# Turning only the normed tokens of a block, by products with the identity into both halves of the partitions

## The chip, the cores and the metric

The kernel runs on one core of one Trainium2 chip. The metric is the device time of one execution in microseconds: three runs of the kernel before took 3504.92, 3515.65 and 3518.93 us, median 3515.65. The profile is of a fourth execution, which took 3525.21 us.

## The reference

The input is a batch of 32 images of 56 x 56 pixels with 64 channels, in fp32. The last of three stages is the one that matters here, a mixture of experts over all 100,352 tokens:

```python
x = x + relu(conv3x3(group_norm(x), binary_kernel))
t = tokens(x)
t = t + linear_attention(layer_norm(t))          # 8 heads, per pair of images
xf = layer_norm(t)
top_w, top_i = top_k(xf @ Wg + bg, 2); top_w = softmax(top_w)
for e in range(8):
    h = gelu(xf @ W1[e] + b1[e])                 # 64 -> 256
    out = out + w_dense[:, e:e+1] * (h @ W2[e] + b2[e])   # 256 -> 64
t = t + out
```

Every token uses two of the eight experts, so it falls into one of 28 classes (pairs of experts).

## The kernel before, in words

Images are worked on in 16 pairs. For each pair the kernel does the convolution, the attention, the second layer norm and the gate, then sorts the tokens by class and scatters them as rows into a table in device memory (`rows`). A row has 132 columns: 0 to 63 the token itself, 64 to 127 its normed form (`COL_X` to `COL_W`), then the two weights and the token's number. Rows of one class fill blocks of 512 tokens (`BLK`), and each block passes through its two experts.

A block (functions `turn_in`, `hidden`, `outputs`, `turn_out` on TensorE; `turned`, `gelu`, `evacuate` on ScalarE) goes as follows. SyncE loads the block's rows (`xb`, 128 partitions x 4 tokens x 132) and the two experts' weights. `turn_in` transposes four groups of 128 tokens, each a 128 x 128 piece of token and normed token, into one PSUM bank: the normed tokens come out in partitions 64 to 127. `turned` copies that half twice, into partitions 0 to 63 and 64 to 127 of `xts` in SBUF, because the two experts' hidden products use the two halves of TensorE's rows. `hidden` (two halves q of the 256 hidden units) multiplies by W1, ScalarE applies gelu, `outputs` multiplies by W2, `evacuate` copies the result, `turn_out` transposes it back into the same PSUM bank that `turn_in` uses (`TB`), and VectorE combines it with the weights and adds the token. GpSimd scatters the result, four DMAs a block.

There are 224 blocks. 156 of them run in thirteen turns of 12 blocks (the text calls such a turn of the outer loop a TURN), in a fixed order between the steps of the pairs that come behind them: `STEPS` and `BLOCK_STEPS` give every step a place on every engine, and each engine works through its own list in that order, waiting on semaphores. So a block's turn in can stand between steps of the attention or the convolution of another pair. The other 68 blocks run alone in a tail, written out block by block, with functions of their own (`in_tail`, `hidden_tail`, `outputs_tail`, `out_tail`, `tail_x`, `gelu_tail`): there the turn in (L1041) has a PSUM bank of its own, and TensorE's order within a block is hidden product 0, turn in of the next block, output product 0 of the block before, hidden product 1, output product 1, turn out.

Lines: L990 and L1041 turn in, L800 and L801 (turns) and L825 and L826 (tail) the copies to `xts`, L972 and L1023 hidden products, L981 and L1032 output products, L998 and L1049 turn out, L788 and L818 gelu, L884 convolution, L871 turning the input of the convolution, L894 turning its output, L899 and L907 keys, queries and values, L913, L920, L926, L935 the rest of the attention, L942 and L949 the gate's logits, L707 squares of the layer norms. L640 is GpSimd's scatter of results, L634 that of sorted rows.

## Time and profile before

| | us |
|---|---|
| median of three runs | 3515.65 |
| lowest and highest | 3504.92, 3518.93 |
| profiled execution | 3525.21 |
| its span, first to last instruction | 3523.1 |
| TensorE busy | 3018.8 (86%) |
| VectorE busy | 2232.3 (63%) |
| ScalarE busy | 1885.4 (54%) |
| GpSimd busy | 1873.1 (53%) |
| mean granted TensorE clock | 0.914 |

The granted clock is a share of TensorE's full speed; 1.0 is 2.4 GHz and the other level is 0.5. A matmul's busy time in the profile includes the time that its result takes to come out, so the distance from one start to the next says more of TensorE's throughput than the mean duration. The first 700 us have no blocks, 700 to 3130 us hold the thirteen TURNs, and from 3130 us on the tail runs.

### The profile page before, as it was taken

To read this page: it belongs to the slowest core of one execution; us is meant where nothing else is said; L and a number is where in the kernel's file an instruction comes from. 1 tells how busy PE (TensorE), PEld (TensorE's weight loads), DVE (VectorE), ACT (ScalarE), POOL (GpSimd) and SP (SyncE) were. 2 spreads that over 40 slices of the span, in tenths; PEclk is the share of its full clock that TensorE was granted. 3 is DMA by queue.
4 is the path that set the end of the run, shared out by engine and by line. 5 is a ranking of instruction groups with operands and counts; after the bars stand their busy time and mean duration, and the time that the engine had idled before them with its cause. 6 is when DMAs were issued, how large, how long until landed. Compare 5 with 4: busy or idle time off the path is not lost. (4 is left out here: it accounts for less than half of the span.)

```text
span 3523.1 us, 60494 instructions
## 1 busy us (share of the span) xinstructions
PE 3018.8 (86%) x16878; PEld 1610.9 (46%) x16878; DVE 2232.3 (63%) x5060; ACT 1885.4 (54%) x3186; POOL 1873.1 (53%) x1837
## 2 busy tenths in 40 slices
PE   3787787889898989999898989899998977579997
PEld 2554554554544444545445444445454443123332
DVE  3677768676868586767667585867677667122222
ACT  2424243365655556565656465565656445347776
POOL 0006244264646556473737465464747375757777
PEclk8888787899999999999999999899999898889999
DMA  8303313142524252433424252424333222234442
GB/s 224 83 26 108 91 64 102 56 121 69 145 72 134 78 137 82 122 88 99 112 83 129 65 142 70 133 80 119 90 108 93 84 74 57 75 92 132 123 104 61
DMA packets 406811, 345.90 MB, mean 98 GB/s; under 512 B 258189, under 2 KB 347028, under 8 KB 400656
## 3 DMA queue, kind: packets, MB, share of 16 engines
q1 hardware_dynamic: 343632, 260.62, 28.0%
q0 software_dynamic: 53760, 78.84, 6.6%
q10 hardware_dynamic: 9088, 2.47, 0.4%
q8 instruction: 153, 2.51, 0.3%
q14 instruction: 178, 1.46, 0.1%
HBM read 261.66 MB, written 147.47 MB: 116 GB/s over the span
## 5 line engine op out<-in xcount | busy, mean ns | idle before, releaser
L634 POOL DMA_INDIRECT rows<-R,place_at x784 | 802.8, 1024 | 571.7 <-issue 513.7
L640 POOL DMA_INDIRECT out<-o_sb,xb x624 | 664.0, 1064 | 722.5 <-DVE o_sb L1471 406.2
L788 ACT ACTIVATE h_sb<-psum,w2b 128x512 f32<-128x512 f32 x624 | 394.2, 683 | 329.3 <-PE psum L972 327.6
L884 PE MATMUL psum<-xpad,conv_w 128*64 128x448 f32 x2688 | 546.4, 558 | 10.0 <-ACT xpad L717 7.5
L972 PE MATMUL psum<-xts,w1b 64*128 64x512 f32 x1248 | 386.4, 693 | 61.0 <-ACT h_sb L788 31.4
L981 PE MATMUL psum<-h_sb,w2b 128*64 128x512 f32 x1248 | 353.4, 646 | 48.0 <-ACT h_sb L788 47.5
L884 PEld LDWEIGHTS psum<-xpad,conv_w 128*64 128x64 f32 x2688 | 190.5, 140 | 329.0 <-issue 315.0
L640 POOL DMA_INDIRECT out<-o_sb,xpad x272 | 272.0, 1000 | 119.2 <-issue 92.7
L751 ACT ACTIVATE conv_y<-psum 128x448 f32<-128x448 f32 x112 | 60.5, 541 | 367.4 <-PE psum L884 367.4
L907 PE MATMUL psum<-WT,conv_y 128*112 128x256 f32 x896 | 233.8, 393 | 11.6 <-DVE QT L1394 6.5
L616 POOL TENSOR_TENSOR QT<-QT,q_sum 112x512 f32<-112x512 f32 x112 | 120.5, 1082 | 229.3 <-DVE q_sum L1419 228.0
L742 ACT COPY xpad<-psum 128x448 f32<-128x448 f32 x224 | 142.8, 648 | 180.8 <-PE psum L871 179.7
L1483 DVE TENSOR_TENSOR y_w<-psum,xpad 128x512 f32<-128x512 f32 x68 | 47.0, 692 | 270.9 <-PE psum L1049 267.0
L818 ACT ACTIVATE h_sb<-psum,VT 128x512 f32<-128x512 f32 x272 | 172.2, 684 | 79.0 <-PE psum L1032 71.5
L871 PE MATMUL psum<-ident,raw 112*128 112x112 f32 x896 | 145.0, 302 | 80.3 <-DMA raw<-in_x 30.0
L894 PE MATMUL psum<-ident,conv_y 128*64 128x64 f32 x3136 | 198.9, 287 | 12.4 <-DVE x_tok L1378 11.7
L894 PEld LDWEIGHTS psum<-ident,conv_y 128*64 128x64 f32 x3136 | 185.8, 205 | 49.8 <-issue 30.3
L907 PEld LDWEIGHTS psum<-WT,conv_y 128*112 128x112 f32 x896 | 151.7, 179 | 109.9 <-issue 48.9
L972 PEld LDWEIGHTS psum<-xts,w1b 64*128 64x128 f32 x1248 | 104.0, 198 | 212.7 <-issue 157.6
L926 PE MATMUL psum<-KT,VT 112*128 112x128 f32 x896 | 140.1, 314 | 55.3 <-ACT KT L729 55.3
L717 ACT ACTIVATE xpad<-xpad,gn 128x784 f32<-128x784 f32 (+2 forms) x160 | 160.1, 1034 | 30.9 <-DVE gn L1370 30.2
L871 PEld LDWEIGHTS psum<-ident,raw 112*128 112x128 f32 x896 | 107.6, 162 | 142.0 <-issue 75.3
(230 smaller groups left out, 5572.3 us busy)
## 6 DMA issues: line engine op xcount, KB each, us to landing
rows<-rows SPq DMA_DIRECT2D x236, 264.0 KB, 5.8
xb<-rows SPq DMA_DIRECT2D x156, 264.0 KB, 2.7
x_tok<-in_x SPq DMA_DIRECT2D x16, 1568.0 KB, 7.3
w2b<-w2x SPq DMA_DIRECT2D x312, 65.0 KB
w1b<-w1x SPq DMA_DIRECT2D x312, 64.2 KB
xpad<-rows SPq DMA_DIRECT2D x68, 264.0 KB, 2.7
raw<-in_x SPq DMA_DIRECT2D x32, 448.0 KB
raw<-in_x SPq DMA_DIRECT2D x32, 440.0 KB
```

What stands on the lines that cost most here:

```text
L634: pool.indirect_dma_start(rows[:, :], bass.IndirectOffsetOnAxis(ap=place_at[:, j:j + 1], axis=0), R[:, j, :], None) \
L640: pool.indirect_dma_start(out_rows, bass.IndirectOffsetOnAxis(ap=block_rows[:, t, COL_ID:COL_ID + 1].bitcast(U32), axis=0), tokens[:, t, : ...
L717: ins = act.activation(part, part, ACT.Identity, bias=shift[h, :], scale=scale[h, :])
L742: act.copy(dst, src[:, 0:448].rearrange("p (k r h) -> p r h k", k=4, h=2)) \
L788: act.activation(h_sb[:, e, q, :], psum[:, HB0 + e, :], ACT.Gelu, bias=w2b[:, i, e, 2 * C + q:2 * C + q + 1]).then_inc(S["h_ready"], 1)
L818: act.activation(h_sb[:, e, q, :], psum[:, HB0 + 2 * q + e, :], ACT.Gelu, bias=t_w2[:, k % TAIL_RING, e, 2 * C + q:2 * C + q + 1]).then_in ...
L871: ins = pe.transpose(dst[:, TQ * r:TQ * r + TQ], raw[0:TQ, 4 * grp + r, :], ident[0:TQ, 0:TQ])
L884: ins = pe.matmul(dst[64 * i:64 * i + 64, 0:BL], conv_w[:, t, :], xpad[:, i, r0:r0 + ROWS, dx:dx + HW], start=(t == 0), stop=(t == 5))
L894: ins = pe.matmul(dst[h, C * j:C * j + C], cols[:, JB * b + j, :], ident[:, h], start=True, stop=True)
L907: ins = pe.matmul(dst[0:LC, 256 * c:256 * c + 256], t[:, o:o + LC], WT4[:, 0:2, :].rearrange("p w m -> p (w m)"), start=True, stop=True)
L972: ins = pe.matmul(psum[:, HB0 + e, :], w1b[h, i, 128 * q:128 * q + 128], xts[h, i % 2, :], start=True, stop=True)
L981: ins = pe.matmul(psum[64 * e:64 * e + 64, YB, :], w2b[:, i, e, C * q:C * q + C], h_sb[:, e, q, :], start=(q == 0), stop=(q == 1))
```

## The change

`turn_in` and `in_tail` no longer transpose 128 x 128 pieces. For each of the four groups of 128 tokens they take only the 64 normed columns as the stationary operand and the identity as the moving one, and multiply twice: once into partitions 0 to 63 of the PSUM bank and once into 64 to 127. Both halves then hold the turned normed tokens, and ScalarE copies all 128 partitions at once.

```diff
             def turned(q4, i):
                 act.wait_ge(*blocks_done("xt_full", (q4, i), 1, 1))
                 act.wait_ge(*blocks_done("h_full", block_at(q4, i - 2), 2, 2))
-                act.copy(xts[0:C, i % 2, :], psum[COL_X:COL_W, TB, :])
-                act.copy(xts[C:128, i % 2, :], psum[COL_X:COL_W, TB, :]).then_inc(S["xt_free"], 1)
+                act.copy(xts[:, i % 2, :], psum[:, TB, :]).then_inc(S["xt_free"], 1)
...
-                act.copy(xts[0:C, k % 2, :], psum[COL_X:COL_W, T_IN, :])
-                act.copy(xts[C:128, k % 2, :], psum[COL_X:COL_W, T_IN, :]).then_inc(S["t_x_ready"], 1)
+                act.copy(xts[:, k % 2, :], psum[:, T_IN, :]).then_inc(S["t_x_ready"], 1)
...
                 for t in range(BT):
-                    ins = pe.transpose(psum[:, TB, 128 * t:128 * t + 128], xb[:, i, t, 0:COL_W], ident[:, :])
+                    for e in range(2):
+                        ins = pe.matmul(psum[64 * e:64 * e + 64, TB, 128 * t:128 * t + 128], xb[:, i, t, COL_X:COL_W],
+                                        ident[:, :], start=True, stop=True)
                 ins.then_inc(S["xt_full"], 1)
...
                 for t in range(BT):
-                    ins = pe.transpose(psum[:, T_IN, 128 * t:128 * t + 128], t_xb[:, k % TAIL_RING, t, 0:COL_W], ident[:, :])
+                    for e in range(2):
+                        ins = pe.matmul(psum[64 * e:64 * e + 64, T_IN, 128 * t:128 * t + 128],
+                                        t_xb[:, k % TAIL_RING, t, COL_X:COL_W], ident[:, :], start=True, stop=True)
                 ins.then_inc(S["t_x_full"], 1)
```

No step moves; each turn in has other instructions in the same place. This is one block of the tail in TensorE's program before (names: `xpad` holds the loaded rows there, `keys` W1, `VT` W2; shapes are those of the result, partitions x elements):

```order
L1049 MATMUL psum<-ident,y_sb 128x128 x4
L1023 MATMUL psum<-xts,keys 128x512 x2
L1041 MATMUL psum<-ident,xpad 128x128 x4
L1032 MATMUL psum<-h_sb,VT 64x512 x2
L1023 MATMUL psum<-xts,keys 128x512 x2
```

And the same place of the changed kernel, where the lines of the turn in and turn out are L1042 and L1051:

```order
L1051 MATMUL psum<-ident,y_sb 128x128 x4
L1023 MATMUL psum<-xts,keys 128x512 x2
L1042 MATMUL psum<-ident,xpad 64x128 x8
L1032 MATMUL psum<-h_sb,VT 64x512 x2
L1023 MATMUL psum<-xts,keys 128x512 x2
```

The turn in stands where it stood, with eight products in place of four transposes. On ScalarE the same difference in the turns reads (gelu L788, convolution's input copy L742):

```order
-L800 COPY xts<-psum 64x512
-L801 COPY xts<-psum 64x512
+L800 COPY xts<-psum 128x512
 L788 ACT_TABLE_LOAD
 L788 ACTIVATE h_sb<-psum,w2b 128x512 x2
 L742 COPY xpad<-psum 128x56x2x4 x2
-L800 COPY xts<-psum 64x512
-L801 COPY xts<-psum 64x512
+L800 COPY xts<-psum 128x512
```

One copy of 128 partitions stands in the place of two of 64.

## Rows read from the trace of the kernel before

**Rows 1.** The page: busy us, share of the span and instructions of each engine.

```profile
PE 3018.8 (86%) x16878; PEld 1610.9 (46%) x16878; DVE 2232.3 (63%) x5060; ACT 1885.4 (54%) x3186; POOL 1873.1 (53%) x1837
```

**Rows 2.** Line L990: durations min/median/max in ns, first and last start, forms.

```profile
L990 PE MATMUL psum<-ident,xb x624: 270/273/477, 698.4 to 3104.7; 128*128 128x128 f32 x156
```

**Rows 3.** Busy us and instructions by stretch: PE, PEld, DVE, ACT, POOL, clock, DMA.

```profile
1506.00:1525.00 19.00, 18.05 (x73) 9.90 (x73) 17.84 (x56) 14.63 (x23) 14.73 (x15) 1.00 0.29 85
1525.00:1537.00 12.00, 11.99 (x65) 5.32 (x64) 7.10 (x15) 11.91 (x16) 9.19 (x10) 1.00 0.44 119
1537.00:1570.00 33.00, 26.54 (x145) 16.58 (x143) 12.47 (x25) 13.03 (x22) 25.21 (x26) 0.84 0.23 68
1570.00:1584.00 14.00, 14.00 (x74) 6.29 (x72) 11.03 (x20) 8.04 (x16) 7.42 (x7) 1.00 0.29 79
...
1470.00:1664.00 194.00, 176.06 (x1039) 95.18 (x1036) 137.54 (x312) 110.60 (x187) 109.71 (x106) 0.94 0.37 102
...
3000.00:3130.00 130.00, 69.35 (x275) 24.04 (x272) 23.79 (x60) 44.63 (x73) 97.55 (x99) 0.80 0.26 75
3145.00:3505.00 360.00, 355.97 (x1589) 123.18 (x1588) 103.64 (x201) 281.69 (x462) 261.21 (x261) 1.00 0.42 111
```

**Rows 4.** The timeline of one block of the tail: start us, us, engine, line.

```profile
3300.05 0.66 PE L1049 MATMUL psum<-ident,y_sb 128*128 128x128 f32 x4
3300.06 0.58 ACT L826 COPY xts<-psum 64x512 f32<-64x512 f32 x1
...
3300.74 1.13 PE L1023 MATMUL psum<-xts,keys 64*128 64x512 f32 x4
...
3301.80 0.66 PE L1041 MATMUL psum<-ident,xpad 128*128 128x128 f32 x4
...
3302.39 1.08 PE L1032 MATMUL psum<-h_sb,VT 128*64 128x512 f32 x4
...
3304.45 1.08 PE L1032 MATMUL psum<-h_sb,VT 128*64 128x512 f32 x4
...
3305.46 0.66 PE L1049 MATMUL psum<-ident,y_sb 128*128 128x128 f32 x4
```

**Rows 5.** Timelines of TensorE in a TURN: products of 128 and of 448 columns.

```profile
1547.99 1.06 PE L926 MATMUL psum<-KT,VT 112*128 112x128 f32 x8
...
1572.61 4.73 PE L884 MATMUL psum<-xpad,conv_w 128*64 128x448 f32 x24
1577.17 1.03 PE L981 MATMUL psum<-h_sb,w2b 128*64 128x512 f32 x4
1578.13 0.60 PE L913 MATMUL psum<-ident,QT 112*128 112x112 f32 x4
```

**Rows 6.** The same timelines: two turns in and what follows each.

```profile
1583.56 0.60 PE L990 MATMUL psum<-ident,xb 128*128 128x128 f32 x4
1584.00 0.92 PE L935 MATMUL psum<-Q,ctx_m 128*128 128x448 f32 x2
...
1616.86 0.66 PE L990 MATMUL psum<-ident,xb 128*128 128x128 f32 x4
1617.45 4.73 PE L884 MATMUL psum<-xpad,conv_w 128*64 128x448 f32 x24
```

**Rows 7.** Waits of TensorE, 700 to 2800 us: total us, times, longest.

```profile
PE psum L926 <- ACT KT L729: 40.0, 11, 3.6
...
PEld psum L998 <- ACT xts L801: 58.5, 58, 2.2
```

**Rows 8.** Timelines around three waits of TensorE for ScalarE (in brackets: idle before, releaser).

```profile
1487.32 1.97 PE L981 MATMUL psum<-h_sb,w2b 128*64 128x512 f32 x4 [2.87 <-ACT h_sb L788]
...
1587.41 0.58 ACT L707 ACTIVATE ln_sq<-R 128x448 f32<-128x448 f32 x1 [1.15 <-DVE lnv L1157]
...
1589.24 0.66 PE L998 MATMUL psum<-ident,y_sb 128*128 128x128 f32 x4 [1.30 <-ACT xts L801]
...
1635.84 1.08 PE L981 MATMUL psum<-h_sb,w2b 128*64 128x512 f32 x4 [0.47 <-ACT h_sb L788]
```

## The prediction

> **What bounds the kernel now.** I read the page first: TensorE is busy 86% of the span, no other engine over 63%, and TensorE falls quiet only at the two ends [rows 1]. Next I read the duration of one transpose [rows 2], and then busy time by stretch, since a share over the whole span mixes several regimes [rows 3]. The reader should see three things there. In the tail (3145 to 3505 us) TensorE is busy 356 of 360 us: it is the bound. In the twelve turns of some 192 us (TURN below; 700 to 2830 us holds eleven of them) it changes: from 1506 to 1525 us VectorE is as full as TensorE (17.8 and 18.1 of 19 us), from 1537 to 1570 neither is, and from 1570 to 1584 TensorE alone is (14.0 of 14). From 3000 to 3130 us GpSimd, with its DMA issues, is the busiest (97.6 of 130 us) and TensorE has 69: no cost of TensorE shows there. Last I read the waits of TensorE [rows 7, 8] and one block of the tail row by row [rows 4].
>
> **The tail, before.** One block takes 5.41 us (L1049 at 3300.05 to L1049 at 3305.46) [rows 4]. Its pieces on TensorE, start to start: turn out 0.69, hidden 1.06, turn in 0.59, then output, hidden and output product 3.07, of which the last has 1.01. Only one of them holds a wait: the turn out has the same four transposes as the turn in but takes 0.10 more, because the hidden product behind it (L1023, 3300.74) needs the second copy L826, which starts at 3300.06, takes 0.58 and ends at 3300.64. Everything else is back to back.
>
> **What a product costs against a transpose.** A transpose is one TensorE instruction, an fp32 product is two: the program has four products at L926 and the trace eight, twelve at L884 and the trace 24 [rows 5]. Eight passes of 128 columns at L926 take 1.06 us, of which one pass's own duration is 0.27 (that of L990 [rows 2]): seven steps of 0.11. That is also the step of the transposes ((0.66 - 0.27 - 0.05)/3 = 0.11). Products into the two halves of the partitions run two at a time: 24 passes of 448 columns at L884 take 4.56 us until L981 starts, 12 steps of 0.38, and two passes of 448 columns one behind the other would be 0.75. So the eight new products are 16 passes, two at a time, 8 steps of 0.11 = 0.88 us, in place of 4 steps = 0.44. The stationary operand is 64 contiguous columns and is loaded behind the running pass, as at L884.
>
> **What a change of the array's shape costs.** Transposes and one-piece products use the array whole, the new products and L884, L981, L1032 use it in column halves, L972 and L1023 in row halves. Two rows give the price: L990 to L935 (both whole) takes 0.44 us start to start, L990 to L884 (whole to halves) 0.59 [rows 6]. So 0.15 per change: 0.10 of gap and 0.05 for the first load that nothing hides. The page "TensorEngine Tiling (Array Packing)" of the Trainium skill, section "Key Properties", says that changing the tiling mode drains TensorE, without a figure; it speaks against this change wherever whole-array work stands on both sides of the turn. The row above gives the size.
>
> **The sum in the tail.** The order fences show the turn in between a hidden product (row halves) and an output product (column halves). The entry costs the same as before. Inside, +0.44. At the exit, the change of shape goes: -0.15 (L981 behind L884 starts at once and takes 0.96 where L1032 takes 1.01 [rows 4, 5]). So +0.29 us of TensorE per block. The copy that goes (0.58, L826) frees the 0.10 wait: -0.10. ScalarE, busy 282 of 360 us or 4.2 us per block, falls to 3.7, and GpSimd has 3.9 [rows 3]; both stay under the new period of 5.60. Net +0.19 x 67 blocks = **+13 us**. Bounds: +0.17 (11 us) with steps at their shortest; +0.34 (23 us) if the shortcut at the exit doesn't come, because the output product waits for a semaphore in front of its load.
>
> **The sum in the turns.** Twelve turns in each. By what stands beside them in the program: eight have whole-array work on both sides (+0.44 + 0.15 + 0.15 = +0.73), two go from whole to column halves (+0.44 + 0.15 - 0.15), two stand between row and column halves (+0.29): 7.3 us of TensorE per TURN, and ScalarE loses 12 x 0.58 = 7.0 us. What counts is which of it lands where something is waited for:
> - 1446 to 1537 us: six turns in. VectorE is full for most of it and TensorE waits, for instance 2.87 us at 1487 for a gelu that stands behind VectorE's statistics in the chain [rows 8]. I cost the additions at nothing; the cover is VectorE's own queue (stats, centring, queries).
> - 1537 us: the turn in stands right before the longest wait of a TURN, L926 for the copy of keys, 40.0 us in 11 times [rows 7]. Hidden. The two long exponentials that lead to it stand behind the xts copies in ScalarE's queue, which is full there (11.9 of 12 us [rows 3]); one copy less brings them forward by 0.58, less what the hidden product feeding the gelu between is late: -0.3.
> - 1570 us, exposed: +0.73. 1584 us: the wait at L998 (1.30 us) is for L801, whose copies start when ScalarE gets past a square (L707) that waits for VectorE [rows 8]. It swallows the turn in before it (+0.73) and gives back 0.58: -0.58.
> - 1596, 1617, 1632 us: exposed, +0.29, +0.44, +0.29. Two gelus waited for there (0.5 us each, one of them in rows 8, at 1635.84) stand directly behind the xts copies: -1.0. The copies of normed tokens at 1603 us do too: -0.2. The turn in at 1638 has whole-array work on both sides and a wait of the same kind behind it, and I count what is left: +0.15.
> Together -0.3 + 0.73 - 0.58 + 1.02 - 1.0 - 0.2 + 0.15 = **-0.2 per TURN**, times 11 = -2 us. Bounds: +4.4 per TURN if nothing of the 7.3 is swallowed and only the 5.3 waits per TURN at L998 (58.5 us in 58 times [rows 7]) give back 0.55 each: +48 us; below, -3 per TURN if half of the 7.0 us taken from ScalarE lands on the chain: -33 us. I take -2, since rows 3 show both engines full where the additions fall and the waits that absorb them.
>
> **The sum.** +13 - 2 = +11 us on the profiled execution's 3525.21 us, so 3536. The median of the three runs is 3515.65, 9.6 below the profiled one, so I forecast 3527 us, +0.3%. A measurement of this kernel can hardly tell less than 0.5% (17.6 us) from no change.
>
> **Rivals.**
> - A, TensorE sets the pace of the whole TURN. For it: busy 176 of 194 us, and its waits are many and small. Against it: 3-us waits for others before L981 and L926, and a full VectorE. Price: +48 in the turns, +13 in the tail, +61: 3577 us. It decides if more than about a tenth of the 7.3 us that I call hidden in each TURN (0.5 us) comes through. Half of it would be some +35, 3551. This is slower than before.
> - B, ScalarE's queue sets more of the chain than I think: 58 waits of TensorE at L998 for copies of which half goes, and gelus queued behind them. Price: -33 in the turns, +13 in the tail: -20, 3496 us. Against it: in the same stretches VectorE has no gap either. It decides if each TURN gets shorter by 3 us.
> - C, the new products stream as four passes' time each in place of two. By rows: a step of 0.11 for the transposes would be 0.44 for a product pair: +1.31 inside a turn in place of +0.44. Tail +1.06 x 67 = +71, turns (three to four exposed ones more by 0.87) +30: about +100, 3616 us. Against it are the eight passes of L926. The Trainium skill's "TensorE: Matmul & The Clock Gate", section "Terms", calls the transpose mode four times faster for fp32, and this rival is that rule; by the rows the factor is two.
> - That the change doesn't do what it says: the order shows eight products and one copy in each place, so no.
>
> **Chances.** Forecast 0.50 (its own range 3510 to 3550), A with its halves 0.28, B 0.14, C 0.04, 0.04 left for what shifts unseen between queues. Range 3496 to 3572: from B's value to just under A's full price; C and the outer parts of A and B are left out. Faster by over 0.5%: 0.14. Within: 0.52. Slower: 0.34 (A, C, and the end of the forecast at which the exit's shortcut is missing in the tail).
>
> **What would show it.** In the profile after: 16 matmul records per turn in, in pairs, steps of 0.11 us, and 0.9 us from its start to the next group; the xts copy still 0.58 us at 128 partitions; a block of the tail at 5.6 us (5.75 if the exit's shortcut is missing) and no wait left at the hidden product; TensorE's waits at L998 for xts cut by about half; the period of a TURN unchanged to 1 us. The prediction is wrong if the tail's blocks stay at 5.4 (then TensorE was not its bound), or if a TURN is more than 1.5 us longer or shorter.

## The result, and the profile after

| | before | after |
|---|---|---|
| median, us | 3514.0 | 3535.32 |
| lowest and highest | 3496.14, 3532.1 | 3517.13, 3554.73 |
| runs | 19 | 19 |
| ratio to before, 95% interval | | 1.0048 [1.0032, 1.0064] |
| profiled execution, us | 3525.21 | 3517.13 |

The change makes the kernel 0.5% slower: 3514.0 x 0.0048 = 17 us [11, 22]. I forecast 3527 us and +11, and the medians as they stand differ by 21. The two profiled executions stand the other way round (3517.13 after, 3525.21 before), because the one of after is the fastest of its 19 runs. So I take durations and distances from it, and never a difference of its total.

The page of the changed kernel: busy us, share of the span and instructions of each engine.

```profile
PE 3094.0 (88%) x19566; PEld 1690.1 (48%) x19566; DVE 2234.4 (64%) x5060; ACT 1724.4 (49%) x2962; POOL 1872.0 (53%) x1837
```

Against [rows 1] TensorE has 2688 instructions more, which is 12 for each of 224 turn ins, and 75 us more of busy time. ScalarE has 224 instructions and 161 us less. The others did not move. The same instructions one by one (durations min/median/max in ns, first and last start; the turn in is L989 now, in the tail L1042; the copies of turned tokens are L800 and L824):

```profile
L989 PE MATMUL psum<-ident,xb x2496: 269/273/477, 696.4 to 3086.4; 128*64 128x128 f32 x192
...
L1042 PE MATMUL psum<-ident,xpad x1088: 272/273/474, 3110.2 to 3484.2; 128*64 128x128 f32 x182
...
L800 ACT COPY xts<-psum x156: 566/590/636, 697.5 to 3087.4; 128x512 f32<-128x512 f32 x156
...
L824 ACT COPY xts<-psum x68: 584/585/587, 3112.3 to 3486.6; 128x512 f32<-128x512 f32 x68
```

A block's turn in is 16 records (1088 / 68), each as long as a transpose was [rows 2]. A copy of 128 partitions takes 0.585 us, the 0.58 that a copy of 64 took [rows 4].

**The tail.** TensorE's timeline of one block after, with ScalarE's copy (start us, us, engine, line):

```profile
3297.00 0.66 PE L1051 MATMUL psum<-ident,y_sb 128*128 128x128 f32 x4
...
3297.59 1.13 PE L1023 MATMUL psum<-xts,keys 64*128 64x512 f32 x4
...
3298.64 1.09 PE L1042 MATMUL psum<-ident,xpad 128*64 128x128 f32 x16
...
3299.57 1.03 PE L1032 MATMUL psum<-h_sb,VT 128*64 128x512 f32 x4
...
3300.53 1.13 PE L1023 MATMUL psum<-xts,keys 64*128 64x512 f32 x4
...
3301.59 1.08 PE L1032 MATMUL psum<-h_sb,VT 128*64 128x512 f32 x4
...
3301.88 0.58 ACT L824 COPY xts<-psum 128x512 f32<-128x512 f32 x1
...
3302.60 0.66 PE L1051 MATMUL psum<-ident,y_sb 128*128 128x128 f32 x4
```

From L1051 to L1051 it is 5.60 us, as forecast, and each piece moved as forecast: turn out to hidden 0.59 (0.69 in [rows 4]: the wait for the second copy is gone), turn in 0.93 (it was 0.59), the output product behind it 0.96 (it was 1.01, since its first load hides now). The copy ends long before its reader. Busy time over a steady part of the tail (TensorE, its loads, VectorE, ScalarE, GpSimd, clock, DMA share, GB/s), before:

```profile
3145.00:3480.00 335.00, 332.32 (x1483) 115.23 (x1484) 94.87 (x184) 263.71 (x433) 242.25 (x242) 1.00 0.45 118
```

and after:

```profile
3145.00:3480.00 335.00, 335.00 (x2158) 137.40 (x2158) 93.88 (x180) 214.07 (x360) 240.08 (x240) 1.00 0.43 113
```

ScalarE fell from 264 to 214 of 335 us, GpSimd is as it was, and TensorE is still the bound: it is busy all of the 335 us. First turn in to last turn in of the tail, 67 periods, took 362.1 us before and 373.1 after: +11.0 us, where my sum said +13 (the average period after is 5.57 us, a little under the steady 5.60).

**The TURNs.** Waits of TensorE, 700 to 2800 us, in the profile before, the ones that [rows 7] does not show (total us, times, longest):

```profile
PE psum L981 <- ACT h_sb L788: 41.0, 34, 2.9
...
PE psum L972 <- issue: 29.4, 9, 5.2
PE psum L913 <- POOL QT L616: 27.5, 20, 2.0
...
PE psum L998 <- ACT xts L801: 17.5, 16, 1.4
```

And after, in the same stretch (L979 was L981, L911 was L913, L924 was L926, L970 was L972):

```profile
PE psum L911 <- POOL QT L616: 39.9, 24, 3.0
PE psum L979 <- ACT h_sb L788: 23.2, 12, 2.2
PE psum L924 <- ACT KT L729: 21.3, 11, 1.9
PE psum L970 <- issue: 21.2, 9, 3.4
...
PEld psum L998 <- ACT xts L800: 14.6, 18, 0.8
```

The waits for copies of turned tokens fell from 58.5 to 14.6 us (I had said by half; it is three quarters). Those are waits of the weight loads (PEld), part of which the matmuls before them cover; TensorE itself was idle there for 17.5 us before, and after no such row is left. The waits for gelus fell from 41.0 to 23.2, those for the keys from 40.0 to 21.3, and those for GpSimd's queries rose from 27.5 to 39.9. TensorE's busy time in the same 2100 us, before and after:

```profile
700.00:2800.00 2100.00, 1902.60 (x11004) 1031.47 (x11006) 1480.58 (x3342) 1206.40 (x2041) 1187.47 (x1143) 0.94 0.36 102
```

```profile
700.00:2800.00 2100.00, 1964.62 (x12721) 1076.71 (x12720) 1494.97 (x3371) 1112.31 (x1917) 1195.67 (x1149) 0.95 0.37 103
```

So its idle time fell from 197 to 135 us: TensorE's longer turn ins were paid for in the main out of its own waits.

The row "issue" was new to me: TensorE is idle some 3 us once a TURN, at the hidden product that starts at 1456.62 us before, and no engine releases it. The trace holds records of branches too, and one of them stands there. In TensorE's program TURNs 2 to 10 are one loop (L410), and its sequencer has nine compare-and-branch instructions, one at the end of each round. In the profile before, the eight that jump back take 4.3 to 6.7 us each (4.67 us from 1451.57), and each ends 0.4 to 0.5 us before that hidden product starts; the ninth, which leaves the loop, takes 0.08 us. The other engines' branches take 0.04 to 0.07 us. So this idle time is the loop's jump back on TensorE. The profile after has 3.6 to 4.8 us for the eight. Why TensorE's jump takes so long, no run shows.

The length of a TURN, start of its first turn in to the next one's, is the measure for the rest. A steady TURN, without a stretch of low granted clock behind its turn in at 1596, takes 191.3 us before (the one that starts at 1447) and 191.0 to 191.2 after (five in a row). The forecast said -0.2 a TURN. But not every TURN without such a stretch is like it: in the profile before the five of TURNs 2 to 10 take 187.5, 188.7, 191.3, 191.2 and 189.4 us. The steady TURN isn't the average one, as the last experiment shows.

### The profile page after: what moved, and what is told of

The parts are those of the page before. It is cut to its first block, busy times and chain, and to the rows that moved or that the text cites. A ratio compares the mean times of both kernels' runs of the same rounds, so it can differ in the third digit from the quotient of the medians.

```text
span 3515.1 us, 65646 instructions
## 1 busy us (share of the span) xinstructions
PE 3094.0 (88%) x19566; PEld 1690.1 (48%) x19566; DVE 2234.4 (64%) x5060; ACT 1724.4 (49%) x2962; POOL 1872.0 (53%) x1837
## 4 chain that ended last, share of the span: by engine, by line
PE 38%; POOL 25%; DVE 16%; issue 15%; ACT 2%; DMA 2%; SPq 2%; POOLq 0%; DVEq 0%; ACTq 0%
POOL rows L634 16%; PE psum L882 8%; POOL out L640 8%; PE psum L1023 4%; PE psum L970 4%; PE psum L1032 4%; PE psum L947 3%; PE psum L979 3%; PE psum L933 2%; PE psum L940 2%; PE psum L1042 2%; PE psum L989 2%; ACT xpad L717 1%; DVE lnv L1152 1%; POOL QT L616 1%
## 5 line engine op out<-in xcount | busy, mean ns | idle before, releaser
L788 ACT ACTIVATE h_sb<-psum,w2b 128x512 f32<-128x512 f32 x624 | 393.9, 684 | 350.6 <-PE psum L970 349.5
L882 PE MATMUL psum<-xpad,conv_w 128*64 128x448 f32 x2688 | 536.7, 550 | 10.0 <-ACT xpad L717 7.5
L970 PE MATMUL psum<-xts,w1b 64*128 64x512 f32 x1248 | 385.9, 693 | 31.3 <-issue 22.0
L979 PE MATMUL psum<-h_sb,w2b 128*64 128x512 f32 x1248 | 352.3, 644 | 29.5 <-ACT h_sb L788 29.3
L742 ACT COPY xpad<-psum 128x448 f32<-128x448 f32 x224 | 142.9, 649 | 200.2 <-PE psum L869 199.7
L989 PE MATMUL psum<-ident,xb 128*64 128x128 f32 x2496 | 181.8, 290 | 58.7 <-DMA xb<-rows 41.7
L869 PE MATMUL psum<-ident,raw 112*128 112x112 f32 x896 | 147.2, 305 | 81.8 <-DMA raw<-in_x 28.6
L989 PEld LDWEIGHTS psum<-ident,xb 128*64 128x64 f32 x2496 | 143.9, 144 | 112.8 <-issue 61.0
L970 PEld LDWEIGHTS psum<-xts,w1b 64*128 64x128 f32 x1248 | 103.1, 197 | 184.9 <-issue 165.6
```

The lines of the kernel that those rows point to most:

```text
L788: act.activation(h_sb[:, e, q, :], psum[:, HB0 + e, :], ACT.Gelu, bias=w2b[:, i, e, 2 * C + q:2 * C + q + 1]).then_inc(S["h_ready"], 1)
L869: ins = pe.transpose(dst[:, TQ * r:TQ * r + TQ], raw[0:TQ, 4 * grp + r, :], ident[0:TQ, 0:TQ])
L882: ins = pe.matmul(dst[64 * i:64 * i + 64, 0:BL], conv_w[:, t, :], xpad[:, i, r0:r0 + ROWS, dx:dx + HW], start=(t == 0), stop=(t == 5))
L970: ins = pe.matmul(psum[:, HB0 + e, :], w1b[h, i, 128 * q:128 * q + 128], xts[h, i % 2, :], start=True, stop=True)
L979: ins = pe.matmul(psum[64 * e:64 * e + 64, YB, :], w2b[:, i, e, C * q:C * q + C], h_sb[:, e, q, :], start=(q == 0), stop=(q == 1))
L989: ins = pe.matmul(psum[64 * e:64 * e + 64, TB, 128 * t:128 * t + 128], xb[:, i, t, COL_X:COL_W], ident[:, :], start=True, stop=True)
```

## Experiments

Twelve runs, in three groups of four. The first group (the change split in four ways) stood against 25 runs of the kernel before, median 3516.11 us, the second against 23, median 3515.32 us; the third was for the traces.

**The change in the tail alone, and in the TURNs alone.** The diff of the change was split between its halves. For the tail alone (`tail_x` and `in_tail`):

```diff
-                act.copy(xts[0:C, k % 2, :], psum[COL_X:COL_W, T_IN, :])
-                act.copy(xts[C:128, k % 2, :], psum[COL_X:COL_W, T_IN, :]).then_inc(S["t_x_ready"], 1)
+                act.copy(xts[:, k % 2, :], psum[:, T_IN, :]).then_inc(S["t_x_ready"], 1)
...
-                    ins = pe.transpose(psum[:, T_IN, 128 * t:128 * t + 128], t_xb[:, k % TAIL_RING, t, 0:COL_W], ident[:, :])
+                    for e in range(2):
+                        ins = pe.matmul(psum[64 * e:64 * e + 64, T_IN, 128 * t:128 * t + 128],
+                                        t_xb[:, k % TAIL_RING, t, COL_X:COL_W], ident[:, :], start=True, stop=True)
```

For the TURNs alone the same two edits stand in `turned` and `turn_in`, with `psum[:, TB, ...]` and `xb`, and the tail is as before.

> Only the tail has the change (products and one copy); the twelve blocks of a TURN are as before. Theory (TensorE is the bound of the tail, the TURNs absorb their part): a block of the tail takes 5.60 us in place of 5.41, its turn in 0.93 us start to start, no wait at the hidden product behind the turn out; the TURNs as before; the whole +12 to +13 us, a ratio of 1.0036. If the whole change's 21 us came from the tail alone this would be 1.006; if they came from the TURNs, 1.000 with a tail that is no slower.

> Only the blocks in the TURNs have the change; the tail is as before. Theory: within 5 us of before (ratio 0.999 to 1.002), the tail's blocks at 5.41 us. Rival A (TensorE sets the pace of a TURN): +48 us, ratio 1.014. Rival B (ScalarE's queue sets it): -33 us, ratio 0.991.

Measured: the tail alone 3526.63 us, ratio 1.0037 [1.0016, 1.0058], +13 us [6, 20]. The TURNs alone 3530.26 us, ratio 1.0032 [1.0012, 1.0053], +11 us [4, 19]. The tail's part is what I forecast, 5.60 us a block (L1050 at 3304.27 and at 3309.87). The middle of the TURNs' part is outside my +-5 us (the interval just reaches into it), and far under rival A's +48. So a part of the result was not in my sum, and its place is in the TURNs.

**The products with two copies.** ScalarE's two copies of 64 partitions are back, from the changed kernel:

```diff
-act.copy(xts[:, i % 2, :], psum[:, TB, :]).then_inc(S["xt_free"], 1)
+act.copy(xts[0:C, i % 2, :], psum[COL_X:COL_W, TB, :])
+act.copy(xts[C:128, i % 2, :], psum[COL_X:COL_W, TB, :]).then_inc(S["xt_free"], 1)
```

> TensorE's part alone, in TURNs and tail: the products are there, but ScalarE still copies twice, each time from the upper half of the bank. Theory: the tail goes by the loop of gelu, two copies, hidden product, turn in, output product, so by 5.41 + 0.29 = 5.70 us a block (+20 us), where TensorE alone would allow 5.60; in the TURNs the waits at L998 stay, and what ScalarE gave back is missing: +1.5 to +2.5 us each, together +35 to +48, ratio 1.010 to 1.014. Rival A: 7.3 us more in each TURN, +100, ratio 1.028. Rival B (only ScalarE's time counts in the TURNs): +20 in all, ratio 1.006.

Measured 3554.09 us, ratio 1.0115 [1.0083, 1.0146], +40 us. One block of its tail:

```profile
3305.04 0.66 PE L1053 MATMUL psum<-ident,y_sb 128*128 128x128 f32 x4
3305.74 1.13 PE L1025 MATMUL psum<-xts,keys 64*128 64x512 f32 x4
3306.80 1.09 PE L1044 MATMUL psum<-ident,xpad 128*64 128x128 f32 x16
3307.72 1.03 PE L1034 MATMUL psum<-h_sb,VT 128*64 128x512 f32 x4
3308.68 1.13 PE L1025 MATMUL psum<-xts,keys 64*128 64x512 f32 x4
...
3310.75 0.66 PE L1053 MATMUL psum<-ident,y_sb 128*128 128x128 f32 x4
```

The 0.70 from turn out to hidden is back and the turn in stays at 0.92: 5.71 a block. So the second copy alone costs the tail 0.11 a block. Of the +40 us the tail has 19 (381.4 us from its first turn in to its last, against 362.1) and the first TURN 8 (186.4 us against 178.5 in the profile before); the rest is in the other TURNs. Five of these take 191.0 to 191.4 us, no more than the steady TURN of before: by that measure alone the missing copy would cost a TURN nothing, where I had expected +1.5 to +2.5. Over the ten TURNs from the second to the eleventh it is +1.4 each (the table at the end of this section).

**One copy with the transposes.** The transposes stay, ScalarE copies the 128 turned columns once (this leaves out a part of what is computed: the first expert works on the tokens in place of the normed ones).

```diff
-act.copy(xts[0:C, i % 2, :], psum[COL_X:COL_W, TB, :])
-act.copy(xts[C:128, i % 2, :], psum[COL_X:COL_W, TB, :]).then_inc(S["xt_free"], 1)
+act.copy(xts[:, i % 2, :], psum[:, TB, :]).then_inc(S["xt_free"], 1)
```

> ScalarE's part alone, in TURNs and tail: the transposes of 128 x 128 stay and ScalarE makes one copy of all 128 partitions, so that the first expert of a block works on the tokens in place of the normed ones (this is what the kernel computes otherwise than the reference). Theory: the tail loses only the wait of 0.10, 5.31 us a block (-7 us); a TURN gets 1.5 to 2.5 us shorter, together -24 to -34, ratio 0.990 to 0.993. Rival A (TensorE sets the TURN, its waits at L998 give back 0.55 each): -2.9 per TURN, -39 in all, 0.989. Rival B: -3 to -7 per TURN, -40 to -80, 0.977 to 0.989.

Measured 3495.99 us, ratio 0.9953 [0.9937, 0.997], -17 us [-22, -11], less than forecast. Its tail is as forecast (354.5 us in place of 362.1, 5.32 a block), and its undisturbed TURNs take 187.6 us, -3.7. Over ten TURNs that would be -37, where the ratio leaves -9 for them. Most of this is the measure: 191.3 us is the steady TURN of before and not the average one. TURNs 2 to 11 without what they lose to low clock at 1596 and 1617 (the last experiment) sum to 1879.0 us here against 1895.6, -1.7 each. That leaves -17 against -9; three of its eleven TURNs lose 17 us there in all (the traces of before 23), so low clock at that place is not what is missing. Its twelfth TURN is 3.5 us longer (179.9 against 176.4); the rest stays open.

**The second copy's wait taken away in another way.** The tail's two copies go to VectorE, all else as before:

```diff
-                act.copy(xts[0:C, k % 2, :], psum[COL_X:COL_W, T_IN, :])
-                act.copy(xts[C:128, k % 2, :], psum[COL_X:COL_W, T_IN, :]).then_inc(S["t_x_ready"], 1)
+                dve.tensor_copy(xts[0:C, k % 2, :], psum[COL_X:COL_W, T_IN, :])
+                dve.tensor_copy(xts[C:128, k % 2, :], psum[COL_X:COL_W, T_IN, :]).then_inc(S["t_x_ready"], 1)
```

> As before, but the tail's two copies of a turned block are made by VectorE in place of ScalarE. Theory: VectorE's copy is shorter than ScalarE's 0.58 us and it is less than half busy in the tail, so the wait of 0.10 at the hidden product goes: the block takes 5.31 us, -7 us, ratio 0.998. Rival: if the 0.10 is not the wait for the second copy but a step of TensorE itself, the block stays at 5.41, ratio 1.000.

Measured 3507.76 us, ratio 0.997 [0.9955, 0.9986], -11 us [-16, -5]. The line view of the copies, and TensorE's timeline of one turn out and one turn in:

```profile
L1474 DVE COPY xts<-psum x68: 692/692/694, 3116.6 to 3471.5; 64x512 f32<-64x512 f32 x68
L1475 DVE COPY xts<-psum x68: 694/694/696, 3117.3 to 3472.2; 64x512 f32<-64x512 f32 x68
```

```profile
3303.91 0.66 PE L1045 MATMUL psum<-ident,y_sb 128*128 128x128 f32 x4
3304.50 1.13 PE L1019 MATMUL psum<-xts,keys 64*128 64x512 f32 x4
3305.56 0.66 PE L1037 MATMUL psum<-ident,xpad 128*128 128x128 f32 x4
3306.14 1.08 PE L1028 MATMUL psum<-h_sb,VT 128*64 128x512 f32 x4
```

The turn out takes 0.59, the wait is gone, and the tail 354.7 us in place of 362.1. VectorE's copy is not shorter than ScalarE's, as I had expected, but longer (0.69 against 0.58 us); it is in time because VectorE has room (with the copies it is busy 184 us of the 335 from 3145 to 3480). This version beats both kernels: it takes the gain that the change made in the tail without its price.

**Products of the whole array.** The transposes of before are replaced by four products with the same 128 columns, two copies as before:

```diff
-ins = pe.transpose(psum[:, T_IN, 128 * t:128 * t + 128], t_xb[:, k % TAIL_RING, t, 0:COL_W], ident[:, :])
+ins = pe.matmul(psum[:, T_IN, 128 * t:128 * t + 128], t_xb[:, k % TAIL_RING, t, 0:COL_W], ident[:, :],
+                start=True, stop=True)
```

> The transposes are replaced by four products of the whole array (128 columns of stationary operand, so 2 x 4 passes one behind the other), and the two copies stay. TensorE never changes shape for it more than before. Theory: the two passes of a product can't run beside each other's half, so 8 steps of 0.11 as in the changed kernel, but with the shape changes of before: tail 5.41 + 0.44 = 5.85 us a block (+29 us); the turn-ins with whole-array work on both sides cost +0.44 in place of +0.73, those at the exit into column halves +0.44 too, and no copy goes, so an undisturbed TURN takes 191.3 + 5 x 0.44 = 193.5 (+24 us): ratio 1.015. If the price of a shape change (0.15) is wrong and such changes cost nothing, the tail's block takes 5.70 us here as with the half products and two copies (which took 5.70), and the ratio is near its 1.0115.

Measured 3586.0 us, ratio 1.0194 [1.0169, 1.0219], +68 us. TensorE's timeline of one block of the tail:

```profile
3301.36 0.66 PE L1051 MATMUL psum<-ident,y_sb 128*128 128x128 f32 x4
3302.06 1.13 PE L1024 MATMUL psum<-xts,keys 64*128 64x512 f32 x4
3303.12 1.16 PE L1042 MATMUL psum<-ident,xpad 128*128 128x128 f32 x8
3304.21 1.08 PE L1033 MATMUL psum<-h_sb,VT 128*64 128x512 f32 x4
3305.22 1.13 PE L1024 MATMUL psum<-xts,keys 64*128 64x512 f32 x4
...
3307.29 0.66 PE L1051 MATMUL psum<-ident,y_sb 128*128 128x128 f32 x4
```

Eight passes one behind the other take 1.09 us until the output product starts; the sixteen passes in column halves, two at a time, took 0.93. This is the price of leaving whole-array work for column halves, 0.16, as the 0.15 between the two rows of [rows 6]. But the output product behind them takes 1.01 here and 0.96 there, so with it the price is 0.21, where my sum had 0.15 for both together. And eight passes in place of four transposes cost 1.09 - 0.59 = 0.50 us, where I had 0.44. The block takes 5.93 us, 0.08 above the 5.85 expected and 0.22 above the 5.71 of the products in halves with two copies, and over the 67 periods 395.1 - 362.1 = 33 us, 0.49 each. The page "TensorEngine Tiling (Array Packing)" of the Trainium skill (section "Key Properties") says that a change of tiling mode drains TensorE, and gives no figure; these rows agree, and here it costs the 0.21 us.

**The products twice.** From the changed kernel, each turn in of the TURNs issues its eight products twice over:

```diff
-                for t in range(BT):
+                for t in (0, 1, 2, 3, 0, 1, 2, 3):
```

> The changed kernel, with the eight products of every turn-in in the TURNs issued twice over (the tail is unchanged): a slope measurement. Each of 12 turn-ins of a TURN gets 0.88 us more of TensorE. Theory (of them only those at 1570, 1596, 1617, 1632 and partly 1603 and 1638 are exposed, the others fall into waits): an undisturbed TURN goes from 191.1 to 195 us (four to five times 0.88), 11 x 3.9 = +43 us over the changed kernel; with its own 1.005 a ratio of 1.017. Rival A (TensorE paces all of it): 12 x 0.88 = 10.6 a TURN, +116 us, ratio 1.038. Rival B (ScalarE's queue paces it): under +1 a TURN, ratio 1.007.

Measured 3620.14 us, ratio 1.0302 [1.0278, 1.0326], +106 us over before and +85 over the changed kernel's median. Its steady TURNs take 199.4 to 200.0 us; the one of the table below takes 199.5, 8.4 above 191.1, of 12 x 0.88 = 10.6 added. That is between my forecast (+3.9) and rival A's, nearer to A's. Where it came through is seen between the turn ins. The table is worked out from the starts of the turn ins in the traces: us from the turn in at that time (of the TURN that starts at 1447 in the profile before) to the next one, in a TURN without low clock there.

```
                              1525  1570  1584  1596  1617  1632
before                        12.1  13.9  12.8  20.5  15.2   6.1
transposes, one copy          12.1  13.9  12.1  20.5  14.6   5.6
products, two copies          12.8  14.6  12.8  20.7  15.4   6.3
after: products, one copy     12.8  14.6  12.2  20.7  14.8   6.0
products only from 1584 on    12.1  14.0  12.2  20.7  14.8   5.9
whole-array products          12.4  14.3  12.8  21.0  15.7   6.1
products twice                13.6  15.5  13.0  21.6  15.7   6.9
```

The last row is 0.8 to 0.9 above "after" in every column: there TensorE's added time counts in full. Together they hold 5.2 of the 8.4 (the interval from 1537, which is not in the table, changes with the clock in it). The rows above price the two halves of the change by themselves: in these six intervals, 80.6 us before, the products cost +2.0 and the copy that goes gives back 1.5 with the products (82.6 to 81.1) and 1.8 with the transposes. The rest of the 8.4 lies in 1447 to 1525, where I had called it hidden (+4.4, less 1.2 at 1537), and 2 us of it is this row of its waits, the jump back of the loop, 700 to 2800 us:

```profile
PE psum L970 <- issue: 40.1, 9, 5.3
```

40.1 in 9 times, where the changed kernel had 21.2 in 9. (Its eight jumps take 5.8 to 6.7 us.)

**Products only where the sum found a gain.** The products and the one copy at the four turn ins from 1584 to 1632 of each TURN, transposes and two copies at the other eight; in the tail the transposes with VectorE's copies:

```diff
-                    turn_in(*block_at(q4, i + 1))
+                    turn_in(*block_at(q4, i + 1), slot in HALVES_AT)   # HALVES_AT = (7, 8, 9, 10)
```

> The products with one copy are kept only at the turn-ins of slots 8 to 11 of a TURN (where my sum found a gain of 0.6, 0.2, 0.4 and 0.1 us); elsewhere and in the tail the transposes are back, and the tail's two copies are made by VectorE, which has room there. Theory (my sum by places): the tail's block takes 5.31 us in place of 5.41 (the 0.10 wait for the second copy goes), so -7 us; an undisturbed TURN takes about 190.3 us in place of 191.3, so -11 us; -18 us in all, ratio 0.995, a little less if the long slots 9 and 10 fall in low-clock stretches more often. Rival A (every us of TensorE counts): four turn-ins cost +0.59 each, +2.4 us a TURN, +26 us, less 7: ratio 1.005. Rival B (ScalarE's queue counts everywhere): 4 x 0.58 = -2.3 us a TURN, -25 - 7: ratio 0.991.

Measured 3519.4 us, ratio 1.0003 [0.9986, 1.002]: not faster, where -18 us was expected. The tail gave its 7 us (354.9), the four intervals their 0.6, -0.2, 0.4 and 0.2 (the table). But TensorE's waits, 700 to 2800 us, have a row, the first of these two, that no other kernel has at this size (the whole-array products have 4.1 us in six times):

```profile
PE psum L894 <- issue: 20.8, 8, 3.6
PE psum L972 <- issue: 20.3, 9, 2.7
```

And its timeline at the start of one TURN:

```profile
1850.88 1.13 PE L972 MATMUL psum<-xts,w1b 64*128 64x512 f32 x4 [2.56 <-issue]
1851.93 1.60 PE L894 MATMUL psum<-ident,conv_y 128*64 128x64 f32 x22
1856.27 0.71 PE L894 MATMUL psum<-ident,conv_y 128*64 128x64 f32 x6 [2.73 <-issue]
```

The idle time without a releaser comes twice there, 20.3 + 20.8 = 41 us in place of 29.4, +12 us. The first is at the loop's jump back, which ends at 1850.50. The second comes some 5 us later and cuts a row of 28 like instructions in two (22 and 6), so it belongs to no wait of the program and to no branch. The clock took the rest: in seven of its eleven TURNs the interval from 1596 is 23.8 or 25.8 us long in place of 20.7, and with the next interval that is 31 us, 9 more than the traces with the TURNs of before lose there on average (22.7, below). -18 + 12 + 9 = +3, where the ratio says +1 [-5, +7]; the 9 are those of a single trace.

**The same kernels again, for their traces.** Unchanged copies, one execution each: three of after, one of before.

> The changed kernel once more, for its trace. The intervals between the turn-ins at 1596, 1617 and 1632 us (20.5 and 15.2 us long before, 20.7 and 14.8 after) become 25.6 and 18.0 when a stretch at the lower granted clock falls into them. Theory L: the change makes this more frequent, in 4 or more of 11 TURNs on average over the traces of the changed kernel, against 4.7 (5, 6 and 3) in the three traces with the TURNs of before; the rest of the 11 TURNs then sums as in the kernel before (2071 to 2076 us without the time lost in those two intervals). Rival M: the frequency is the same, and the rest of the TURNs is longer by 8 to 11 us: 2080 to 2085 us, as it was 2081.2 in the first trace of the changed kernel.

> As the run before it: the same kernel, for a further count of TURNs with and without a low-clock stretch at 1596 to 1632 us. Theory L: over the traces of the changed kernel the time lost in those two intervals averages 8 us more than the 27 us of the three traces with the TURNs of before (32.6, 35.8, 12.0). Rival M: it averages 27 us or less, and the rest of the 11 TURNs is 2080 us or more.

> As the two runs before it, the same kernel and the same count. Both theories expect the same base TURN, 191.1 us, and the tail at 5.60 us a block; they differ in where the other 8 to 11 us are.

> The kernel before once more, for its trace, to have as many traces of its TURNs. Both theories: base TURN 191.3 us, the rest of the 11 TURNs 2071 to 2076 us without the time lost in the two intervals at 1596 to 1632 us; that loss between 10 and 36 us.

Measured: 3545.32, 3528.01 and 3563.72 us for after, 3502.64 for before (beside them a further execution of before took 3527.12). With tail_only and tail_dve (whose TURNs are those of before) there are four traces of TURNs as before, and with turns_only five as after. From the starts of the turn ins, in us:

```
                      TURN 1   TURNs 2 to 11   of these, lost at 1596 and 1617   the rest
before                178.5    1925.2          32.5                              1892.7
tail_only             176.9    1934.4          35.8                              1898.6
tail_dve              178.8    1908.1          12.0                              1896.1
before_again_1        178.3    1905.4          10.4                              1895.0
after                 183.7    1904.6           0.7                              1903.9
turns_only            185.1    1930.9          32.3                              1898.6
after_again_1         183.4    1927.4          24.4                              1903.0
after_again_2         185.1    1913.2           6.8                              1906.4
after_again_3         185.0    1947.7          42.2                              1905.5
```

"Lost" is what the intervals from 1596 and from 1617 have above their lengths in the table of intervals. Three things are seen.

First, in TURNs 2 to 11 that loss is no larger with the change (mean 21.3) than without (22.7), though with 10 to 36 us in four traces and 1 to 42 in five the means could hide several us either way: theory L is not borne out there. (Over all eleven, in the order of the table, 5, 6, 3 and 3 TURNs lose time there, and with the change 1, 9, 8, 3 and 11, always the first among them.) Over all eleven TURNs, as both theories were put, the loss is 6 us larger with the change (28.6 against 22.7), all of it the first TURN's, and the rest is 7 us longer (2080.6 against 2073.7): each of the two has about half.

Second, the rest of the ten TURNs is longer with the change, 1903.5 against 1895.6 on average, **+7.9 us** (one trace of each kind has the same 1898.6). Ten steady TURNs would have made it 2 shorter, so some 10 us have to be found, and two places have them. The four intervals from 1447 to 1506 sum to 583 us in place of 580, where ten steady TURNs would have been 2 shorter: 5 us. The interval at 1537 has 6. The steady TURN has that interval at 32.5 us before and 32.1 after, with 10 us of low clock in it. But with 7 us of low clock or less it is mostly 30.5 before, and after it is mostly 31.1 with 7 and 30.0 with 3 to 4. Over ten TURNs it sums to 314.0 us before and 315.9 after, where steady TURNs would have made it 4 shorter; the low clock in it sums to 76 us before and 84 after. My reading, not shown by a run of its own: the wait for the keys that hid some low clock there is the one that fell from 40.0 to 21.3 us.

Third, the first TURN is longer in every trace with the change, 184.5 against 178.1 on average, **+6.4 us**, with no overlap. It is in one place, the granted clock behind the tenth turn in (at 833 us). Busy time by stretch of before_again_1 (us, PE, PEld, DVE, ACT, POOL, clock, DMA share, GB/s):

```profile
845.00:848.00 3.00, 3.00 (x26) 2.90 (x25) 2.13 (x6) 2.85 (x8) 0.00 (x0) 1.00 0.00 0
848.00:851.00 3.00, 3.00 (x24) 2.14 (x22) 1.04 (x4) 1.23 (x5) 1.65 (x2) 1.00 0.06 16
...
854.00:861.00 7.00, 7.00 (x36) 2.29 (x34) 6.14 (x13) 2.45 (x6) 0.00 (x0) 1.00 0.31 82
```

And of after_again_1:

```profile
845.00:848.00 3.00, 3.00 (x26) 2.89 (x24) 2.21 (x6) 2.72 (x8) 0.00 (x0) 0.98 0.00 0
848.00:851.00 3.00, 3.00 (x15) 2.20 (x12) 0.87 (x3) 1.10 (x3) 1.82 (x2) 0.50 0.03 11
...
854.00:861.00 7.00, 7.00 (x35) 4.89 (x36) 2.50 (x6) 1.84 (x3) 0.00 (x0) 0.50 0.31 84
```

From 842 to 848 us the engines do nearly the same, then the clock falls to 0.50 (1.2 GHz) in the one and stays at 1.00 (2.4 GHz) in the other, and it comes back between 860 and 865 us in the five traces. TensorE was busy without a break from 833 us on in both, with small products of 16 columns and transposes in turn, whose loads (PEld 2.9 of 3 us) fill its time. In the 8 us before that it had 1.1 us of idle time before and none here; but one copy with transposes has none either, and keeps its clock. The stretch makes the interval 25.5 to 25.9 us long in place of 20.5, and the next one 16.3 to 17.8 in place of 15.2. It is tied to the products, not to the copies: products with two copies have it as well (25.9 and 18.2), one copy with transposes does not (20.5 and 14.6). Fewer or other products have a shorter one (23.8 with products only from 1584 on, 22.6 with whole-array products, undisturbed 20.7 and 21.0). It is not the added TensorE time as such either, since the products twice have none of it in their first TURN (21.6, their undisturbed length).

With these sums the two halves of the change can be priced over TURNs 2 to 11, without the losses (one trace each for the middle two, where traces with the same TURNs differ by up to 8):

```
                             the rest   first TURN
before (four traces)         1895.6     178.1
transposes, one copy         1879.0     175.7
products, two copies         1909.3     186.4
after (five traces)          1903.5     184.5
```

They do not simply add. The products cost 13.7 us with two copies and 24.5 with one; the copy that goes gives back 16.6 with the transposes and 5.8 with the products. That fits a common store of waits: what one of the two uses up, the other cannot use again.

## Why the prediction was right, and which steps were off

- **The tail, +13:** right by mechanism and size. 5.60 a block, every piece as forecast. That it came out to the hundredth has some luck in it: by the whole-array products the added passes cost 0.50 and not 0.44, and the exit saves 0.21 and not 0.15, and the two errors of 0.06 cancel. The total was +11.0 in the traces, and the tail alone measured +13 us [6, 20].
- **A product costs two passes of a transpose's step, two at a time in the halves:** shown by the 0.93 (0.92 with two copies) and, without the halves, by 1.09. Rival C (0.44 a pair of products) is out: the turn in would have taken over 1.75 us. The Trainium skill's "TensorE: Matmul & The Clock Gate" ("Terms") gives the transpose mode a factor of four for fp32; the measurement decides, and it is two here. That there are eight products in place of four costs no further time, since they go two at a time.
- **The change of the array's shape, 0.15:** right in kind, too small by 0.06 at the tail's exit. It measured 0.16 up to the start of the output product and 0.05 in it.
- **The copy that goes, -0.10 a block:** shown from three sides: one copy with transposes (5.32), VectorE's copies (0.59), and two copies with products (5.71).
- **The TURNs, -0.2 each:** right for the steady TURN (191.3 and 191.1), and step by step so from 1537 on. At 1537 -0.4 (forecast -0.3), at 1570 +0.7 (+0.73), and from 1584 to 1638 -0.6 + 0.2 - 0.4 - 0.1 = -0.9, where the steps made -0.58 + 1.02 - 1.0 - 0.2 = -0.76. At 1446 to 1537 it was right only since errors cancelled. "I cost the additions at nothing; the cover is VectorE's own queue" failed for the turn ins at 1461 and 1525, which came through with +0.7 each. They were given back by the interval from 1447 (14.3 to 13.5), in which the loop's jump back idles TensorE for 21.2 us in nine times in place of 29.4, -0.9 a TURN. I had not read that row in the waits at all. It goes with the copy more than with the products: 18.9 us with transposes and one copy, 25.5 with products and two.
- **"Times 11 = -2 us":** this step failed. The TURN that I took the prices from was multiplied by eleven, and the first TURN (+6.4) and the average one of the other ten (+0.8, by the traces) are not like it. The first difference and part of the second lie in how the change meets stretches of low clock, for which the sum had no term; the other part is in the four intervals from 1447 to 1506. The twelfth TURN, which the sum left out, cost nothing (176.4 us before and 176.8 after, on average).
- **The total:** 11.0 + 6.4 + 7.9 = 25 us by the means of the traces, 24 with the difference of the losses (-1.4). The medians say 21, and the ratio 17 [11, 22]. The losses alone differ by 25 us (before) and 41 us (after) from trace to trace, so four and five traces can't settle these few us. What makes the clock fall in the first TURN at 848 us with the products and not with the transposes stays open.
- **Rival A (TensorE paces the TURN):** wrong for the change, but nearer the truth than I gave it. The doubled products show that 80% of what is added on top of the change comes through (8.4 of 10.6). The change itself did not cost that, since it met TensorE's waits first: with the copies kept, 14 us of the 73 that I counted for ten TURNs came through, and the copy gave 6 of them back. In the six intervals of the table the two were +2.0 and -1.5 a TURN. I argued that the additions fall where TensorE waits. Most did; the next ones had no such room.
- **Rival B (ScalarE's queue):** right by mechanism (waits for copies down from 58.5 to 14.6 us), wrong as a forecast of the time, for the same reason. And the 58.5 us in 58 times from which the bounds of A and B were counted are waits of weight loads, where TensorE itself was idle for only 17.5 us in 16 times.
- **The time:** 3535.32 lies 8 us above the forecast of 3527 and inside the likeliest case's own range, 3510 to 3550.

## What to carry to other kernels

When a change takes time from one engine and gives it to another in the same chain, price both sides as exposed first and look at the two effects alone: here +2.0 and -1.5 to -1.8 in 81 us, whose sum near zero looked like "hidden". Where both feed on the same waits, measure the two together as well, since the copy was worth 17 us by itself and 6 beside the products. Check also the first period, and idle time that no engine releases, since a price taken from one steady period has neither. And if the aim is only to take a copy off a queue, ask first whether an idle engine can make it: that gave 0.3% where the cleverer turn cost 0.5%.

## What the runs showed of the hardware that was not expected

- The spread of single executions (3496 to 3532 us before, 3517 to 3555 after) is made in large part in one place: a stretch at the lower granted clock that falls into the intervals from 1596 and 1617 or does not. The interval from 1596 takes 20.5 us without one and 22.0 to 25.7 with one (before), and a TURN without one is often followed by others equal to it within 0.2 us (five in a row in the profile after). It cost 33 us in one trace of before and 10 in the next, of the 22.6 us by which their executions differ (3525.21 and 3502.64).
- More load on TensorE made the mean granted clock higher (0.916 before, 0.920 after, 0.932 with the products twice) and the time none the better: what counts is where the low stretch falls.
- The loop's jump back takes TensorE 3.3 to 7.3 us in these traces and leaves it idle for 2 to 6 of them, where the same branch takes 0.08 us when it leaves the loop, and 0.04 to 0.07 on the other engines in the profile before. Waits of 700 to 2800 us have it as "issue": 27.6 to 29.4 us in nine times before, 19.7 to 21.3 after, 40.1 with the products twice. After a jump a second idle time of this kind can follow within some 10 us, in the middle of 28 like instructions (20.8 us in eight times) or of a turn in (3.1 us in the profile after). The runs do not say why the jump takes so long, nor what the second one is.
- A copy of 64 partitions and one of 128 take ScalarE the same time (0.58 us), VectorE needs 0.69.
